# The experts' loop in another order: the row search in two halves, the result scaled on ScalarE

## The reference, cut to what matters

```python
token_buf = jnp.zeros((E * CAP,), jnp.int32).at[buf_idx].set(tok_of_pair, mode='drop')
w_buf = jnp.zeros((E * CAP,), x.dtype).at[buf_idx].set(w_of_pair.astype(x.dtype), mode='drop')
xb = x[token_buf].reshape(E, CAP, H)
gu = jnp.einsum('ech,ehf->ecf', xb, W_gate_up)
g, u = jnp.split(gu, 2, axis=-1)
inter = jax.nn.silu(g) * u
yb = jnp.einsum('eci,eih->ech', inter, W_down)
yb = yb * w_buf.reshape(E, CAP, 1)
routed = jnp.zeros((T, H), x.dtype).at[token_buf].add(yb.reshape(E * CAP, H))
```

## Time and profile before

| | us |
|---|---|
| median of 3 runs | 965.81 (965.38 to 967.29) |
| the profiled execution, its own time | 962.72 |
| its span | 960.9 |
| TensorE busy | 858.6 (89% of the span) |
| VectorE busy | 764.0 (80%) |
| ScalarE busy | 331.0 (34%) |
| GpSimd busy | 292.2 (30%) |
| mean granted clock of TensorE | 0.951 |

### The profile page before, as it was taken

One profiled execution on the slowest core, in us unless ns is written; L12 is line 12 of the kernel. 1 busy time (PEld: TensorE's weight loads), 2 busy tenths in 40 slices (PEclk: granted clock), 3 DMA queues, 4 the chain that ended last, 5 costly groups with the idle time before them and its releaser, 6 DMA issues.

```text
span 960.9 us, 22157 instructions
## 1 busy us (share of the span) xinstructions
PE 858.6 (89%) x7603; PEld 780.6 (81%) x7603; DVE 764.0 (80%) x3778; ACT 331.0 (34%) x931; POOL 292.2 (30%) x350
## 2 busy tenths in 40 slices
PE   1788899899899899899899999999989999999993
PEld 1677688888788798798799999988788888888882
DVE  4266899999899899899999896987744767767773
ACT  0335554453453553553553535231101111111110
POOL 6021212312312412412412311121102555455544
PEclk8798999999999999999999999999986999979997
DMA  6410010100010010110110000111113555545541
GB/s 201 127 50 1 2 42 12 38 28 22 27 32 22 26 33 19 29 31 21 29 31 26 22 19 27 30 28 35 41 40 80 145 139 142 131 118 141 141 101 29
DMA packets 48663, 54.25 MB, mean 56 GB/s; under 512 B 8981, under 2 KB 41595, under 8 KB 48540
## 3 DMA queue, kind: packets, MB, share of 16 engines
q1 hardware_dynamic: 39372, 44.23, 15.8%
q0 software_dynamic: 6592, 7.28, 4.5%
q10 hardware_dynamic: 2608, 1.60, 0.7%
HBM read 42.40 MB, written 10.69 MB: 55 GB/s over the span
## 4 chain that ended last, share of the span: by engine, by line
DVE 39%; PE 33%; DMA 8%; issue 8%; POOL 5%; ACT 3%; SPq 2%; DVEq 0%; POOLq 0%; ACTq 0%
DVE b_arena L1494 9%; DMA out_rows<-b_hid,b_add_index 4%; PE p_big L687 3%; DMA out_rows<-b_inner,b_add_index 3%; PE p_big L688 3%; DVE b_top_a L1480 3%; PE p_shared L832 2%; POOL b_arena L1760 2%; PE p_shared L833 2%; POOL out_rows L1790 2%; PE p_shared L838 2%; DVE b_top_d L1480 2%; DVE b_rstd L1232 2%; DVE b_top_c L1480 2%; PE p_small L694 2%
## 5 line engine op out<-in xcount | busy, mean ns | idle before, releaser
L1538 DVE TENSOR_TENSOR b_arena<-b_iota_b,b_slot 128x1152 bf16<-128x1152 bf16 (+1 forms) x46 | 85.4, 1859 | 7.6 <-issue 7.6
L1760 POOL DMA_INDIRECT b_arena<-x_rows,b_index x44 | 51.0, 1158 | 125.2 <-issue 71.4
L687 PE MATMUL p_big<-b_xT,b_ff1a 128*128 128x128 f32 x384 | 78.5, 288 | 1.2 <-ACT b_xT L1026 1.2
L688 PE MATMUL p_big<-b_xT,b_ff1b 128*128 128x128 f32 x384 | 77.6, 285 | 0.0
L1694 POOL TENSOR_TENSOR b_arena<-b_kY,b_mask_k 64x256 f32<-64x256 f32 x16 | 9.8, 610 | 206.5 <-ACT b_kY L1051 206.5
L687 PEld LDWEIGHTS p_big<-b_xT,b_ff1a 128*128 128x128 f32 x384 | 62.5, 203 | 2.5 <-ACT b_xT L1026 2.5
L1026 ACT COPY b_xT<-p_small 128x256 f32<-128x256 f32 (+1 forms) x97 | 35.5, 377 | 83.4 <-PE p_small L678 83.1
L1725 POOL TENSOR_TENSOR b_arena<-b_arena 128x768 f32<-128x768 f32 x16 | 27.0, 1690 | 117.6 <-DVE b_arena L1506 117.6
L688 PEld LDWEIGHTS p_big<-b_xT,b_ff1b 128*128 128x128 f32 x384 | 61.9, 203 | 0.0
L998 PE MATMUL p_big<-b_xeT,b_arena 128*116 128x192 f32 x320 | 60.7, 333 | 0.0
L721 PE MATMUL p_big<-b_arena,b_q_blk 128*128 128x256 f32 (+3 forms) x256 | 48.9, 334 | 12.5 <-ACT b_q_blk L1058 12.4
(11 more groups left out here) (367 smaller groups left out, 2646.3 us busy)
## 6 DMA issues: line engine op xcount, KB each, us to landing
b_arena<-in_w_gate_up SPq DMA_DIRECT2D x20, 464.0 KB
b_arena<-in_w_down SPq DMA_DIRECT2D x20, 336.0 KB
b_xp<-in_xp SPq DMA_DIRECT2D x16, 384.0 KB, 3.0
b_arena<-in_w_gate_up SPq DMA_DIRECT2D x40, 116.0 KB
xT_rows<-b_xmT SPq DMA_DIRECT2D x16, 128.0 KB, 1.8
b_xT_late<-xT_rows SPq DMA_DIRECT2D x16, 128.0 KB, 2.2
h_rows<-b_h SPq DMA_DIRECT2D x16, 96.0 KB, 1.6
x_rows<-b_xm SPq DMA_DIRECT2D x32, 48.0 KB, 2.0
```

The lines of the kernel that those rows point to most:

```text
L687: mm(o, ff1a[:, c * 128:(c + 1) * 128], xTa[s][:], start=True, stop=False)
L688: last = mm(o, ff1b[:, c * 128:(c + 1) * 128], xTb[s][:], start=False, stop=True)
L1538: last = tt(hot[s][:, tiles, :], iota_b[:, None, :].to_broadcast([128, n, CAP]), slot[:, tiles, bass.ds(e, 1)].to_broadcast([128, n, CAP]) ...
L1760: G.indirect_dma_start(xg[s][:, h, :], None, x_rows[:, :], bass.IndirectOffsetOnAxis(index[s][:, h:h + 1], 0)).then_inc(S(f"gathered{s}"), 16)
```

## The change

The loop on three engines is written in another order; the work is the same.

TensorE: the 17 products for half 0 of the places follow the first up round, the 17 for half 1 the second, and the transposes come behind them. The down products run over the chunks of round 0 for both halves first, which needs only `einner0`, then over those of round 1. ScalarE: it scales the result, behind its copy of the transposes. VectorE: no scaling any more, and the factor 0.5 goes into the copy of the weight. Several pairs of semaphores of the start and of the loop are merged into one with higher counts (`esilu0` and `esilu1` into `esilu`, `index_a` and `index_b` into `index_part`, seven of the class token into three), and two that nobody waited for are gone.

```diff
+            def slots_half(s, v, h):
+                if h == 0:
+                    pe.wait_ge(S("hot_ready"), v)
+                for t in range(NT):
+                    last = mm(lists_bank[s][0:HS, 400 + 6 * h:406 + 6 * h], hot[s][:, t, h * HS:(h + 1) * HS], rhs[s][:, t, :],
+                              start=(t == 0), stop=(t == NT - 1))
+                if h == 1:
+                    last.then_inc(S("index_mm"), 1)
...
                         last.then_inc(S(f"eup{r}"), 1)
+                        slots_half(s, v + 2, r)
                     gathered(1 - s, 32 * i + 32 + 32 * s, v + 1)
-                    slots_of(s, v + 2)
                     pe.wait_ge(S("y_done"), v)
-                    pe.wait_ge(S("einner0"), v + 1)
-                    pe.wait_ge(S("einner1"), v + 1)
-                    for h in range(2):
-                        for c in range(NIC):
-                            last = mm(aux[s][0:HS, h * D:(h + 1) * D],
-                                      einner[s][:, c, h * HS:(h + 1) * HS], w_dn[s][:, c, :],
-                                      start=(c == 0), stop=(c == NIC - 1))
+                    for r in range(2):
+                        pe.wait_ge(S(f"einner{r}"), v + 1)
+                        for h in range(2):
+                            for c in range(2 * r, 2 * r + 2):
+                                last = mm(aux[s][0:HS, h * D:(h + 1) * D],
+                                          einner[s][:, c, h * HS:(h + 1) * HS], w_dn[s][:, c, :],
+                                          start=(c == 0 and h == 0), stop=(c == NIC - 1 and h == 1))
...
                     rows_in(1 - s, v + 1)
+                    act.wait_ge(S("kept"), v)
+                    act.wait_ge(S("down_mm"), v + 2)
+                    for h in range(2):
+                        last = f(y[s][:, h, :], aux[s][0:HS, h * D:(h + 1) * D], ACT.Copy, scale=add_w[s][:, h:h + 1])
+                    last.then_inc(S("y_done"), 1)
...
-                    V.tensor_copy(add_w[s][:], slot_w[s][:]).then_inc(S("kept"), 1)
+                            ts(add_w[s][:], slot_w[s][:], 0.5, None, op0=ALU.mult).then_inc(S("kept"), 1)
...
-                    dve.wait_ge(S("down_mm"), v + 2)
-                    for h in range(2):
-                        last = ts(y[s][:, h, :], aux[s][0:HS, h * D:(h + 1) * D], add_w[s][:, h:h + 1], 0.5,
-                                  op0=ALU.mult, op1=ALU.mult)
-                    last.then_inc(S("y_done"), 1)
```

More of the change, by code:

```diff
@@ L535, in tower_kernel @@
         presets, pool_presets = sem("presets"), sem("pool_presets")
[L536 to L538 removed]
+        cls_products, cls_copies, cls_vectors = (sem("cls_" + n) for n in ("products", "copies", "vectors"))
         named = {name: sem(name) for name in SEMAPHORES.split()}
@@ L892, in second_ff @@
                 if v == 1:
[L893 removed]
+                    pe.wait_ge(cls_copies, 3)
                 if v > 2:
@@ L923, in class_tile @@
                 yield from router(1, 1, B, xTa[1][:, 0:B], xTb[1][:, 0:B])
-            def slots_of(s, v):
-                pe.wait_ge(S("hot_ready"), v)
-                for h in range(2):
-                    for t in range(NT):
-                        last = mm(lists_bank[s][0:HS, 400 + 6 * h:406 + 6 * h], hot[s][:, t, h * HS:(h + 1) * HS], rhs[s][:, t, :],
-                                  start=(t == 0), stop=(t == NT - 1))
-                last.then_inc(S("index_mm"), 1)
+            def slots_half(s, v, h):
[6 more added lines that the diff above has]
+                    last.then_inc(S("index_mm"), 1)
+            def slots_of(s, v):
+                slots_half(s, v, 0)
+                slots_half(s, v, 1)
             def gathered(s, gather_value, v):
@@ L1062, in attention @@
                     rows = slice(64 * g, 64 * g + 64)
-                    last = cp(v_pair[n][v % 2][rows, :, :, g * VD:g * VD + DH],
+                    cp(v_pair[n][v % 2][rows, :, :, g * VD:g * VD + DH],
                               small[s][rows, 0:D].rearrange("p (g h d) -> p g h d", g=2, d=DH))
-                last.then_inc(S(f"at{n}_v_sb"), 1)
                 if n == 1:
@@ L1632, in _ @@
                             .then_inc(S(f"einner{r}"), 1)
[L1634 to L1644 removed]
+                        if r == 1:
+                            dve.wait_ge(S("add_done"), v)
+                            V.tensor_copy(add_index[s][:], index[s][:])
+                            ts(add_w[s][:], slot_w[s][:], 0.5, None, op0=ALU.mult).then_inc(S("kept"), 1)
+                            dve.wait_ge(S("kept"), v)
+                            indices_of(s, v + 2)
+                        if r == 0:
+                            next(slots)
+                    run(slots)
         @block.gpsimd
```

63 lines of the change are left out of this document (26 added, 37 removed).

## The result

| | before | after | ratio, 95% interval |
|---|---|---|---|
| median | 965.52 (20 runs) | 960.37 (20 runs) | 0.9941 [0.992, 0.9962] |
| span of the profiled execution | 960.9 | 958.7 | |
| mean granted clock of TensorE | 0.951 | 0.956 | |

The kernel is faster by 0.6%, some 5 to 6 us. The forecast was -12.5 us. The time lies inside the range of 946.5 to 961, but the gain came out less than half as large as forecast.

What follows compares the result with a forecast made beforehand. A loop of up products, weights burst, scatter landing, gather and transposes bounds the kernel. Period 9.46 + 0.24 = 9.7 us against 10.53 saves 13.3 over sixteen, net -12.5: 965.8 to 953.3 us, range 946.5 to 961.

Steps and rivals of the forecast that it cites:

- The two legs: Experts' loop: TensorE's leg 8.53 us plus the leg through weights burst and gather 10.4, two periods, so 9.46 each.
- Part (1): TensorE's search split around the second up round: its leg falls from 9.48 to 8.53 us, 0.1 us added for switches.
- Part (2): Down products need only `einner0` for their first eight: the wait of 0.3 us goes.
- Part (3): First search half waits for VectorE's `hot_ready`: 1.7 us to spare, about 1 us for the second comparison.
- Part (4): Result scaling moved from VectorE to ScalarE: 0.65 us for two, bounds 0.2 to 1.0, hidden.
- Part (5): GpSimd's collisions with VectorE's comparisons: first scatter stretched by 0.7 us or less, hidden by over 0.5 us to spare.
- The excess of 0.24: Remainder per period for lowered clocks and collisions after the change, with two of seven lowered stretches expected; period 9.7 us.
- the 0.59: Excess per period before the change, put to lowered clocks and GpSimd's collisions with VectorE: measured 10.53 us against 9.94.
- full gain: Rival: no excess remains, GpSimd lands ahead of the burst, period 9.3, 18.9 us less, 947 us; chance 0.05.
- no gain: Rival: GpSimd's chain of gathers and scatters is its own loop, 10.5 us with collisions; 965.8 us; chance 0.09.
- Clock: TensorE's down products: two of the seven lowered stretches expected to remain after the change.
- slower: Rival: thin products between up rounds lower TensorE's clock in 16 of 20 experts, +8.3 us, 974 us; chance 0.06.

Runs made afterwards that it cites:

- a_down_back: Changed kernel with the down products in the old order, waiting for both halves of the hidden values before the first product; 975.07 us, ratio 1.011.
- a_cut_first: Changed kernel with only VectorE's first comparison of a search (6 tiles) cut into three pieces of two tiles; 943.54 us, ratio 0.9818.
- a_gate: Changed kernel with SyncE issuing gate/up weight loads only after TensorE has passed its wait for the gathered rows; 965.58 us, ratio 1.003.
- a_hold: Changed kernel with VectorE's first comparison waiting for a semaphore that GpSimd's program raises behind both gathers; 953.99 us, ratio 0.9926.
- a_hold2: Changed kernel with VectorE's first comparison waiting for a 1x1 memset that GpSimd's engine executes behind both gathers; 955.16 us, ratio 0.9914.

## Why the prediction was wrong, step by step

- **The two legs**: right. 9.39 us for an ordinary pass, where 9.46 stood in the text. The scatter's landing sets the gather in most passes.
- **Part (1)**, search in two halves: right. The row between the rounds costs no idle time of TensorE (0.0 in the groups by line for the search and for the up products behind it), and TensorE's own pass is 9.08 to 9.12 us (9.28 forecast).
- **Part (2)**, the split of the down products: right in its sign and in that no wait is left; too small as a price. I gave it the 0.3 us that the old order waited. In the new order its absence costs 23.3 us of waits (a_down_back), of which 15.9 lie in the seven passes with the late Tanh.
- **Part (3)**, `hot_ready`: right, the search between the rounds waits for VectorE in two passes, 0.3 us at most.
- **Part (4)**, scaling: right. 0.82 us a pass on ScalarE (two of 0.41), 0.65 forecast, hidden.
- **Part (5)**, the collisions, is the step that failed. It said that afterwards "GpSimd runs later against TensorE, so the first scatter starts inside the comparison, at a cost of 0.7 or less", and that this is hidden. The direction was right, and in seven passes the first scatter is what is hit, for up to 1.0 us. That wasn't fully hidden either: the 0.5 us to spare were less than the stretch. The chain of waits of the changed kernel leads through such a scatter into the first accident:

```profile
799.46 2.40 POOL out_rows L1792
...
802.17 3.95 DMA out_rows<-b_inner,b_add_index
...
808.65 5.06 DMA b_arena<-x_rows,b_index
```

  In 11 of the 12 accidents of the four kernels that have them, the first scatter of the pass before was hit (2.1 to 2.6 us). That the one leads to the other is read from the rows and from a_cut_first, not tested by itself. And above all I moved the phase to one place and asked only what stands there. It isn't one place: it varies from pass to pass over several microseconds, and 1.3 us further along the same shift lies the second gather, which isn't hidden, since TensorE's transposes wait for it and the weights burst lies right behind. A stretch of 1 us there lets the burst go first and becomes a wait of 3.4 us, and the clock falls behind it.
- **The excess of 0.24** in the sum thus had two errors against each other. Without an accident nothing of the 0.59 is left: 9.39 us, the "full gain" rival's period of 9.3. With three accidents in 16 periods it is 10.37 - 9.46 = 0.91 us. Expected waits "under 3 us in total" were 12.3 us, and behind the first expert three gathers were bound by their index, where none was expected. My rival "no gain" had gather collisions in it, but as they were before.
- **Clock**: 3 lowered groups, two expected. All three stand behind an accident, none behind anything else, so the "slower" rival's thin products between the rounds do no harm.

So the gain of 0.6% is a difference of two larger numbers. In spans: from 960.9 to 941.2 us without accidents (a_cut_first), 19.7 us, of which three accidents take 17.5 back. That leaves 2.2 us in the profiled executions and 5 to 6 us over all runs. By the ratios a_cut_first is 1.2%, some 12 us, ahead of the change (0.9818 against 0.9941), and not 17.5. Whether other executions have fewer accidents wasn't measured.

## What to carry to other kernels

- When an order moves one engine's work against another's, list each instruction of the other engine that the shifted one can now meet, over the whole spread of the phase, and price the worst by who waits for it and what transfer is queued behind.
- A long VectorE instruction next to GpSimd's indirect transfers is better cut into pieces of about 0.5 us. Here this cost 8.8 us of VectorE's time that nobody waited for and brought 18.7 us of span (958.7 to 940.0) in the new order; in the old order the same cut brought 0.3% or nothing.
- A gain that is missing after a reordering can sit in three passes of twenty. Means by line show only that waits grew; the list of single waits shows where.

## What the runs showed of the hardware

- An indirect transfer's issue on GpSimd that starts inside a comparison of VectorE (two operands in SBUF, bf16) takes up to 2.3 us (gather, ordinarily 0.95) or 3.05 (scatter, ordinarily 1.45). The stretch is what is left of the comparison, less 0.13 us: a_gate's five second gathers start with 1.31, 1.22, 1.09, 0.54 and 0.33 us of it left and take 1.17, 1.09, 0.96, 0.41 and 0.20 us longer. With pieces of 0.45 us a gather's issue takes 0.96 to 1.1. It is the single instruction that keeps GpSimd out, not VectorE's being busy. The Trainium skill (SBUF — State Buffer, "Who interferes with whom") calls the pair of ports that the two engines share an exclusive lock, which the first to issue holds for its whole instruction; these rows agree, the release between two instructions included. The same section infers that this kind of instruction, `tensor_tensor`, leaves the generation of descriptors on GpSimd alone. Here the issue of an indirect transfer is held (1.83 us against 0.96), and the measurement decides.
- A semaphore that GpSimd's program raises by itself behind an indirect transfer is seen by VectorE before the engine has started that transfer's issue (a_hold, 0.11 us ahead); one raised by an instruction of the engine isn't (a_hold2).
- A gather of 96 rows whose issue is stretched by 0.9 us, so that the burst of 696 KB starts before it ends, lands with the end of the burst: 4.95 us from its start against 2.42.
- Open: in 8 passes of a_hold2 and 7 of a_down_back, ScalarE's second Tanh and SyncE's next load, which wait for the same semaphore of TensorE, start together 1.6 to 2.5 us after the last up product in the timeline. The trace puts it to no releaser that it can name. I haven't tried to tell whether the products' recorded times or the semaphore are late, and the rest of a_hold2's missing gain hangs on it.
